# Projecting k and v by pairs of batches in the attention loops of a two-layer gated cross-attention kernel

## The reference, cut to what matters

```
x = x + tanh(g)*attention0(layernorm(x), ctx)      # 16 heads of 16 columns
x = x + tanh(g)*moe8(layernorm(x))                 # 8 experts with a capacity, top 1
x = x + tanh(g)*attention1(layernorm(x), ctx, ctx)
x = x + tanh(g)*moe4(layernorm(x))                 # 4 experts, top 2

# attention, for each batch:
q = layernorm(x) @ Wq ; k = ctx @ Wk ; v = ctx @ Wv
out = softmax(q k^T / 4) v @ Wo
```

## Time and profile before

| | value |
|---|---|
| time of the profiled execution | 2127.31 us |
| its span | 2125.5 us |
| TensorE busy | 2039.2 us (96%) |
| VectorE busy | 1756.2 us (83%) |
| ScalarE busy | 1496.7 us (70%) |
| GpSimd busy | 1217.2 us (57%) |
| 300 to 400 us (layer-0 attention): TensorE, VectorE, ScalarE, GpSimd | 97.91, 86.69, 63.84, 80.52 of 100 us |
| 1400 to 1500 us (layer-1 attention): the same | 100.00, 71.53, 67.27, 75.23 of 100 us |
| granted TensorE clock in both | 1.00 |
| DMA share in both | 0.22, 0.23 |

### The profile page before, as it was taken

The page is one execution under the profiler, slowest core; times in us unless marked ns, Lnnn a source line. Parts: engine busy times, 40 slices in busy tenths (PEclk is TensorE's granted clock), DMA queues, the critical chain, the costliest instruction groups (busy, mean ns, idle before and its releaser), DMA issues.

```text
span 2125.5 us, 57822 instructions
## 1 busy us (share of the span) xinstructions
PE 2039.2 (96%) x19788; PEld 1794.9 (84%) x19788; DVE 1756.2 (83%) x4916; ACT 1496.7 (70%) x3234; POOL 1217.2 (57%) x1800
## 2 busy tenths in 40 slices
PE   6999999999699999999799999999999999999997
PEld 5888888888599999999678888888788888888885
DVE  5889888898588888888677777777589999999996
ACT  4666666666478787878466666666668888888885
POOL 5788888878300000000277878877457777777776
PEclk9999999999799999999799999999999999999998
DMA  7555122221366666666422222222101100001000
GB/s 233 189 180 170 62 71 62 64 68 54 147 223 240 229 238 231 237 232 235 158 66 71 71 74 71 71 71 76 47 24 31 31 31 30 30 30 31 31 28 18
DMA packets 151665, 226.12 MB, mean 106 GB/s; under 512 B 20454, under 2 KB 135786, under 8 KB 141036
## 3 DMA queue, kind: packets, MB, share of 16 engines
q1 hardware_dynamic: 145260, 205.99, 28.8%
q0 software_dynamic: 6144, 16.79, 2.6%
HBM read 153.77 MB, written 68.94 MB: 105 GB/s over the span
## 4 chain that ended last, share of the span: by engine, by line
PE 87%; DVE 4%; issue 3%; DMA 2%; POOL 2%; ACT 1%; SPq 0%; POOLq 0%; ACTq 0%; DVEq 0%
PE ps L1254 11%; PE ps L1270 10%; PE ps L1126 10%; PE ps L1025 10%; PE ps L984 8%; PE ps L1111 6%; PE ps L1065 4%; PE ps L1202 3%; PE ps L1214 3%; PE ps L1158 3%; PE ps L1044 3%; PE ps L1059 2%; PE ps L1082 2%; PE ps L1095 2%; DMA slots_d<-rows,slot_s 2%
## 5 line engine op out<-in xcount | busy, mean ns | idle before, releaser
L1406 DVE TENSOR_REDUCE nmax<-ps 128x16 f32<-128x2048 f32 x128 | 292.4, 2284 | 29.7 <-PE ps L1082 29.3
L873 ACT ACTIVATE prob_t<-ps 128x2048 f32<-128x2048 f32 x128 | 240.9, 1882 | 77.5 <-PE ps L1065 77.5
L688 POOL COPY slot_in<-slot_all 128x1 int32<-128x1 int32 x64 | 11.4, 178 | 473.3 <-DMA eo_d<-eo 473.3
L1025 PE MATMUL ps<-w2f,a_t 128*128 128x256 f32 x1024 | 231.7, 379 | 0.3 <-ACT a_t L805 0.3
L1254 PE MATMUL ps<-xgt_hi,w_hl 128*128 128x256 f32 x1248 | 230.4, 283 | 1.0 <-DVE xgt_lo L1671 1.0
L1270 PE MATMUL ps<-w_hl,hid_hi 128*128 128x256 f32 x1248 | 226.9, 284 | 0.0
L1025 PEld LDWEIGHTS ps<-w2f,a_t 128*128 128x128 f32 x1024 | 189.6, 190 | 23.8 <-ACT a_t L805 0.6
L662 POOL TENSOR_TENSOR km_r<-qk,cst 128x512 fp32r<-128x512 f32 x128 | 133.5, 1043 | 126.1 <-ACT qk L863 126.1
L945 ACT ACTIVATE hid<-ps,b_in 128x256 f32<-128x256 f32 x312 | 146.1, 469 | 82.8 <-PE ps L1254 67.5
L1254 PEld LDWEIGHTS ps<-xgt_hi,w_hl 128*128 128x128 f32 x1248 | 195.7, 190 | 1.4 <-issue 1.4
L805 ACT ACTIVATE a_t<-ps,be_in,g_in 128x128 f32<-128x128 f32 x512 | 186.0, 470 | 12.2 <-PE ps L1044 11.3
(11 more groups left out here) (230 smaller groups left out, 6273.8 us busy)
## 6 DMA issues: line engine op xcount, KB each, us to landing
w_raw<-in_w_dram SPq DMA_DIRECT2D x78, 1024.0 KB, 6.8
c_t<-in_ctx_in_dram SPq DMA_DIRECT2D x128, 128.0 KB
x_d<-x SPq DMA_DIRECT2D x128, 128.0 KB, 2.4
slots_d<-zeros SPq DMA_DIRECT2D x12, 1024.0 KB, 6.1
eo_d<-zeros SPq DMA_DIRECT2D x12, 1024.0 KB, 5.6
xg<-slots_d SPq DMA_DIRECT2D x39, 256.0 KB, 2.8
eo_d<-eo SPq DMA_DIRECT2D x39, 256.0 KB, 2.2
x_in<-in_x_dram SPq DMA_DIRECT2D x64, 128.0 KB, 2.2
```

Source lines behind the costliest of these rows:

```text
L873: nc.scalar.activation(prob_t[:].rearrange("p a k -> p (a k)"), scores.rearrange("p a k -> p (a k)"), ACT.Exp, scale=SOFT).then_inc(y["exp ...
L1025: mm = pe.matmul(dst, a_t[:, b.parity, e, c, :], w2f[:, e, c, :], start=False, stop=True, skip_group_check=True)
L1406: nc.vector.tensor_reduce(nmax[:, b.parity, :, 0:4], scores.rearrange("p a (r k) -> p a r k", k=P), AX_X, ALU.max, negate=True).then_inc(y ...
```

## The change

- k is projected for two batches at once, with fp32r products of high and low parts: the weights `wk_hi` and `wk_lo` stand still and 256 columns (two batches) of `c_hi` or `c_lo` move. That is one group of twelve matmuls, at the end of the odd steps, for the batches s+1 and s+2.
- v is projected for two batches in one group of twelve matmuls, at the end of the even steps, for the batches s-2 and s-1. q stays as it was.
- `c_t`, `c_hi` and `c_lo` hold pairs. `c_hi` and `c_lo` are made every second step, 512 columns wide, two steps ahead.
- On ScalarE the turned rows `x_t` are copied first, then (even steps) the k pair or (odd steps) the v pair. q is copied by itself.
- On GpSimd `km_r` waits for the k copy only, `qm` for the q copy.
- `wk_hi` and `wk_lo` are made by ScalarE and VectorE at the start of each loop; TensorE waits for them.

```diff
...
@@ -222,9 +224,9 @@
-c_t = psb("c_t", [P, 4, C, P])
-c_hi = psb("c_hi", [P, 2, C, P], F32R)
-c_lo = psb("c_lo", [P, 2, C, P], F32R)
+c_t = psb("c_t", [P, 2, C, 2, P])
+c_lo = psb("c_lo", [P, 3, C, 2, P], F32R)
+c_hi = psb("c_hi", [P, 3, C, 2, P], F32R)
@@ -235,7 +237,8 @@
-qk = psb("qk", [P, 4, 4, P])
+q_in = psb("q_in", [P, 4, 2, P])
+k_in = psb("k_in", [P, 2, 2, 2, P])
...
@@ -524,11 +527,14 @@
-    b = s + 1
-    if b.within(B):
-        if (b - 4).begun:
-            sp.wait_ge(y["v_done"].of(b - 4), y["v_done"].at(b - 4))
-        sp.dma_start(c_t[:, b.off % 4].rearrange("p c k -> p (c k)"), row(ctx_in, b)).then_inc(y["c_came"].of(b), 16)
+    e = s + 3
+    if e.off % 2 == 0 and e.within(B):
+        if (e - 3).begun:
+            sp.wait_ge(y["c_lo_done"].of(e - 3), y["c_lo_done"].at(e - 3))
+        for t in range(2):
+            b = e + t
+            sp.dma_start(c_t[:, e.off // 2 % 2, :, t, :], row(ctx_in, b).rearrange("p (c k) -> p c k", c=C))\
+                .then_inc(y["c_came"].of(b), 16)
@@ -545,7 +551,7 @@
-        sp.wait_ge(s_wv[n], 2)
+        sp.wait_ge(s_wv[n], 4)
@@ -711,18 +717,18 @@
-        pool.wait_ge(y["qk_out"].of(b), y["qk_out"].at(b, 1))
-        masked(km_r[:, b.parity], qk[:, b.off % 4, 2:4, :]).then_inc(y["km_done"].sem, 1)
+        pool.wait_ge(y["k_out"].of(b), y["k_out"].at(b))
+        masked(km_r[:, b.parity], k_in[:, b.off // 2 % 2, :, b.off % 2, :]).then_inc(y["km_done"].sem, 1)
         if (b - 2).begun:
             pool.wait_ge(y["s2_done"].of(b - 2), y["s2_done"].at(b - 2))
-        masked(qm[:, b.parity], qk[:, b.off % 4, 0:2, :]).then_inc(y["qm_done"].sem, 1)
-    b = s - 1
-    if b.within(B):
-        pool.wait_ge(y["c_hi_done"].of(b), y["c_hi_done"].at(b))
-        if (b - 2).begun:
-            pool.wait_ge(y["v_done"].of(b - 2), y["v_done"].at(b - 2))
-        nc.gpsimd.tensor_tensor(c_lo[:, b.parity], c_t[:, b.off % 4], c_hi[:, b.parity], ALU.subtract)\
-            .then_inc(y["c_lo_done"].sem, 1)
+        pool.wait_ge(y["q_out"].of(b), y["q_out"].at(b, 1))
+        masked(qm[:, b.parity], q_in[:, b.off % 4]).then_inc(y["qm_done"].sem, 1)
+    e = s + 2
+    if e.off % 2 == 0 and e.within(B):
+        r = e.off // 2 % 3
+        pool.wait_ge(y["c_hi_done"].of(e + 1), y["c_hi_done"].at(e + 1))
+        nc.gpsimd.tensor_tensor(c_lo[:, r], c_t[:, e.off // 2 % 2], c_hi[:, r], ALU.subtract)\
+            .then_inc(y["c_lo_done"].sem, 2)
@@ -809,23 +815,31 @@
+nc.scalar.activation(wk_hi[:], w_k[:], ACT.Copy).then_inc(s_wv[n], 1)
 nc.scalar.activation(wv_hi[:], w_vp[:], ACT.Copy).then_inc(s_wv[n], 1)
 def step(s):
-    b = s - 3
-    if b.within(B):
-        act.wait_ge(y["v_done"].of(b), y["v_done"].at(b))
-        if (b - 2).begun:
-            act.wait_ge(y["av_done"].of(b - 2), y["av_done"].at(b - 2))
-        nc.scalar.activation(v_aug[:, b.parity, :, 0:DH], b5[:, 0:D].rearrange("p (h d) -> p h d", h=H),
-                             ACT.Copy).then_inc(y["v_out"].sem, 1)
     b = s
     if b.within(B):
         act.wait_ge(y["x_turned"].of(b), y["x_turned"].at(b))
         if (b - 1).begun:
-            act.wait_ge(y["qk_done"].of(b - 1), y["qk_done"].at(b - 1))
+            act.wait_ge(y["q_done"].of(b - 1), y["q_done"].at(b - 1))
         nc.scalar.activation(x_t[:].rearrange("p a k -> p (a k)"), b7[:, P:P + D], ACT.Copy)\
             .then_inc(y["x_t_done"].sem, 1)
+    e = s
+    if e.off % 2 == 0 and e.within(B):
+        act.wait_ge(y["k_done"].of(e + 1), y["k_done"].at(e + 1))
+        if (e - 3).begun:
+            act.wait_ge(y["s2_done"].of(e - 3), y["s2_done"].at(e - 3))
+            act.wait_ge(y["km_done"].of(e - 3), y["km_done"].at(e - 3))
+        nc.scalar.activation(k_in[:, e.off // 2 % 2].rearrange("p m t k -> p (m t k)"), b5, ACT.Copy).then_inc(y["k_out"].sem, 2)
+    e = s - 3
+    if e.off % 2 == 0 and e.within(B):
+        act.wait_ge(y["v_done"].of(e + 1), y["v_done"].at(e + 1))
+        if (e - 1).begun:
+            act.wait_ge(y["av_done"].of(e - 1), y["av_done"].at(e - 1))
+        nc.scalar.activation(v_aug[:, :, :, 0:DH], b5.rearrange("p (t h d) -> p t h d", t=2, h=H),
+                             ACT.Copy).then_inc(y["v_out"].sem, 2)
@@ -841,13 +855,15 @@
-    b = s - 1
-    if b.within(B):
-        act.wait_ge(y["c_came"].of(b), y["c_came"].at(b))
-        if (b - 2).begun:
-            act.wait_ge(y["v_done"].of(b - 2), y["v_done"].at(b - 2))
-        nc.scalar.activation(c_hi[:, b.parity].rearrange("p c k -> p (c k)"),
-                             c_t[:, b.off % 4].rearrange("p c k -> p (c k)"), ACT.Copy).then_inc(y["c_hi_done"].sem, 1)
+    e = s + 2
+    if e.off % 2 == 0 and e.within(B):
+        r = e.off // 2 % 3
+        act.wait_ge(y["c_came"].of(e), y["c_came"].at(e))
+        act.wait_ge(y["c_came"].of(e + 1), y["c_came"].at(e + 1))
+        if (e - 5).begun:
+            act.wait_ge(y["v_done"].of(e - 5), y["v_done"].at(e - 5))
+        nc.scalar.activation(c_hi[:, r].rearrange("p c t k -> p (c t k)"),
+                             c_t[:, e.off // 2 % 2].rearrange("p c t k -> p (c t k)"), ACT.Copy).then_inc(y["c_hi_done"].sem, 2)
@@ -856,15 +872,14 @@
-        act.wait_ge(y["qk_done"].of(b), y["qk_done"].at(b))
+        act.wait_ge(y["q_done"].of(b), y["q_done"].at(b))
         if (b - 4).begun:
-            act.wait_ge(y["s2_done"].of(b - 4), y["s2_done"].at(b - 4))
             act.wait_ge(y["qm_done"].of(b - 4), y["qm_done"].at(b - 4))
-        nc.scalar.activation(qk[:, b.off % 4].rearrange("p a k -> p (a k)"), b5, ACT.Copy).then_inc(y["qk_out"].sem, 1)
+        nc.scalar.activation(q_in[:, b.off % 4].rearrange("p a k -> p (a k)"), b5[:, 0:2 * P], ACT.Copy).then_inc(y["q_out"].sem, 1)
         if (b - 2).begun:
             act.wait_ge(y["s1_done"].of(b - 2), y["s1_done"].at(b - 2))
         nc.scalar.activation(q_r[:, b.parity].rearrange("p a k -> p (a k)"), b5[:, 0:2 * P], ACT.Copy)\
-            .then_inc(y["qk_out"].sem, 1)
+            .then_inc(y["q_out"].sem, 1)
...
@@ -1120,23 +1135,20 @@
-    def projections(w, part, src):
+    b = s
+    if b.within(B):
+        pe.wait_ge(y["x_t_done"].of(b), y["x_t_done"].at(b))
+        if b.off % 2 == 0:
+            pe.wait_ge(y["k_out"].of(b + 1), y["k_out"].at(b + 1))
+        elif (b - 2).begun:
+            pe.wait_ge(y["v_out"].of(b - 2), y["v_out"].at(b - 2))
+        else:
+            pe.wait_ge(y["q_out"].of(b - 1), y["q_out"].at(b - 1))
         for m in range(C):
             for c in range(C):
-                mm = pe.matmul(b5[:, (part + m) * P:(part + m + 1) * P], w[:, c, m * P:(m + 1) * P],
-                               src[:, c, :], start=(c == 0), stop=(c == C - 1))
-        return mm
-
-    b = s
-    if b.within(B):
-        pe.wait_ge(y["x_t_done"].of(b), y["x_t_done"].at(b))
-        if (b - 3).begun:
-            pe.wait_ge(y["v_out"].of(b - 3), y["v_out"].at(b - 3))
-        elif (b - 1).begun:
-            pe.wait_ge(y["qk_out"].of(b - 1), y["qk_out"].at(b - 1))
-        projections(w_q, 0, x_t)
-        pe.wait_ge(y["c_came"].of(b), y["c_came"].at(b))
-        projections(w_k, 2, c_t[:, b.off % 4]).then_inc(y["qk_done"].sem, 1)
+                mm = pe.matmul(b5[:, m * P:(m + 1) * P], w_q[:, c, m * P:(m + 1) * P], x_t[:, c, :],
+                               start=(c == 0), stop=(c == C - 1))
+        mm.then_inc(y["q_done"].sem, 1)
@@ -1202,18 +1214,29 @@
-    b = s - 2
-    if b.within(B):
-        if (b + 2).within(B):
-            pe.wait_ge(y["qk_out"].of(b + 2), y["qk_out"].at(b + 2))
-        else:
-            pe.wait_ge(y["v_out"].of(b - 1), y["v_out"].at(b - 1))
-        pe.wait_ge(y["c_lo_done"].of(b), y["c_lo_done"].at(b))
-        for c in range(C):
-            for ct, w in ((c_hi, wv_hi), (c_hi, wv_lo), (c_lo, wv_hi)):
-                mm = pe.matmul(b5[:, 0:D], ct[:, b.parity, c, :], w[:, c, :],
-                               start=(c == 0 and ct is c_hi and w is wv_hi), stop=(c == C - 1 and ct is c_lo))
-        mm.then_inc(y["v_done"].sem, 1)
+    if s.off >= 0 and (s.off % 2 == 0 or (s + 1).within(B)):
+        last = s if s.within(B) else At(0, B - 1)
+        pe.wait_ge(y["q_out"].of(last), y["q_out"].at(last))
+    e = s + 1
+    if e.off % 2 == 0 and e.within(B):
+        r = e.off // 2 % 3
+        pe.wait_ge(y["c_lo_done"].of(e + 1), y["c_lo_done"].at(e + 1))
+        for m in range(C):
+            for c in range(C):
+                for w, ct in ((wk_hi, c_hi), (wk_hi, c_lo), (wk_lo, c_hi)):
+                    mm = pe.matmul(b5[:, m * 2 * P:(m + 1) * 2 * P], w[:, c, m * P:(m + 1) * P],
+                                   ct[:, r, c].rearrange("p t k -> p (t k)"),
+                                   start=(c == 0 and w is wk_hi and ct is c_hi), stop=(c == C - 1 and w is wk_lo))
+            mm.then_inc(y["k_done"].sem, 1)
+    e = s - 2
+    if e.off % 2 == 0 and e.within(B):
+        r = e.off // 2 % 3
+        for t in range(2):
+            for c in range(C):
```

(25 more changed lines are left out.)

2 lines of the change are left out of this document (1 added, 1 removed).

## The result

The changed kernel takes 2143.91 us (median of 4 runs, 2141.45 to 2145.79) against 2127.14 (4 runs, 2124.65 to 2129.44): ratio 1.0078, 95% interval 1.0061 to 1.0096. Forecast were 2122 and a range of 2109 to 2134. The profiled execution has a span of 2139.5 us, 14.0 more than before.

A forecast was written before the change was run, and what follows sets the result against it. TensorE, near 98 to 100% busy, was taken as the bound, with VectorE's reduction as floor. Slot cycles -7.4, early steps -1.2, layer 1 +2.4, scatter -0.5, start +1.3 gave -5.4 us: 2122, range 2109 to 2134.

The forecast's parts named there:

- The floor of T: Both loops: T, the maxima transpose's weight load, waits for VectorE's reduction, so not before S (maximum scores' start) + 2.98 us.
- Layer 0's plain step: Layer 0, steps without slot calculation: 7.87 us each, 0.13 less than before.
- The term for the nine early steps: Layer 0, nine steps before the slot work starts: -0.13 us each, -1.2 us in all.
- Layer 1's step: Layer 1, each step: 7.47 us, 0.04 longer than before; +2.4 us over some 60 steps.
- from T to L1158 is 1.55 us ... so 4.49: Layer 1: stretch from the maxima transpose to the next step's start, 4.49 us instead of 4.55 when the transpose is waited for.
- The slot step: Layer 0, step with VectorE's slot calculation: bn_stats at S + 6.75 instead of 7.74; 0.57 us less a cycle, -7.4 us.
- qm from when ScalarE has copied q (about 3.9 ...) to 5.0: Layer 0's slot step, GpSimd layout: qm starts after ScalarE's q copy, about S + 3.9, and ends at 5.0.
- the lower bound of this term: Layer 0's slot cycle if GpSimd is never in VectorE's way: 3 x 7.87 + 8.03 = 31.64 us, -1.34 a cycle.
- The start: Start of layer 0: one more ScalarE copy and VectorE subtraction ahead of the first bn_stats, +1.3 us; layer 1, 0.
- The scatter's wait: Layer 0: scatter issued 1 to 2 us earlier, ending VectorE's wait for its landing; -0.5 us over the loop.
- ScalarE's copies: Both loops: the rearranged, wider copies cost nothing; if 0.2 us later, 0.1 a second step, 6 us in all.
- The rival that came true: VectorE's chain is the loop: reduction floor binds each step, slot chain hardly shortens; 2136 us, chance 0.25.

The follow-up runs named there:

- e1: Changed kernel, with GpSimd's km_r also waiting for VectorE's xh of the same step; 2129.62 us, ratio 1.0013.
- e2: Changed kernel with three buffers for qm instead of two; 2123.50 us, ratio 0.9984.
- b2: Kernel before the change with only ScalarE's order changed, x_t copied in front of v_aug; 2129.33 us, ratio 1.0003.
- e7: Changed kernel with three qm buffers, layer 1's o_pad turn ahead of the maxima's, and ScalarE's wide copy back in front of x_t; 2114.60 us, ratio 0.9937.
- b1: Kernel before the change with three buffers for qm instead of two and nothing else; 2127.79 us, ratio 0.9996.
- e4: Changed kernel; in layer 1 alone TensorE's turn of o_pad stands ahead of the turn of the row maxima; 2148.03 us, ratio 1.0097.
- e6: Changed kernel with three qm buffers, layer 1's early o_pad turn, and layer 0's context pairs split one step earlier; 2123.07 us, ratio 0.9974.

## Why the prediction was wrong, by its steps

- **The floor of T** was right: S + 2.97 or 2.98 in the plain steps of layer 0 and in 52 of 63 steps of layer 1. In layer 1 it has the reduction as releaser, with 0.19 us of wait where I had said some 0.28. In the other eleven T is S + 3.20 to 3.47. Two of these are the first of the loop, and nine lie behind VectorE's one-off weight work, which I had called covered and which is not.
- **Layer 0's plain step**, 7.87: right to the hundredth. The term for the nine early steps was not: -1.2 forecast, -0.1 measured from 56.78 to 113.58, since one of them (from 104.91) took 8.66 in place of 8.00. No run tells why.
- **Layer 1's step**, 7.47: right in even steps (7.42), wrong in odd ones (7.78). The step that failed is "from T to L1158 is 1.55 us ... so 4.49": I took the stretch behind T as TensorE's work alone. It holds a wait for VectorE in each odd step. Term: +2.4 forecast, +9 measured. e1 and e2 each bring the odd step back to 7.46.
- **The slot step.** It is the sentence "qm from when ScalarE has copied q (about 3.9 ...) to 5.0". The copy was there at S + 3.6, but the buffer was free only at S + 4.72. Term: -7.4 forecast, 0 measured. With the wait removed (e2) bn_stats is at S + 6.47, earlier than the forecast 6.75, and the cycle is shorter by 1.0, more than the forecast 0.57. c_lo cost 1.30, not 1.04. The 8.03 in the lower bound of this term has no working: by the prediction's own 5.09 from T to S, the third step was to be about 8.23, as it is in every trace, and the bound 31.84, not 31.64.
- **The start**: +1.3 forecast, +5.1 measured. The first S is 1.3 later (19.95 against 18.68), as forecast, though not by the forecast work alone: the first bn_stats is 2.0 later (11.81 us against 9.81), because wk_lo took 1.75 us beside GpSimd's c_lo, where it took 0.68 in e2. There bn_stats is at 9.85 and the first S at 18.46, no later than before, and the sixth S is still at 55.35. So the other 3.9 lie in the first steps: 7.38, 7.80 and 6.76 us, where they were 4.45, 6.63 and 7.01. I priced the preparation and left out these steps: the first now holds a k pair of 2.5 us behind the turn of xh, and stretches of low clock lie in both. How much each costs is not shown.
- **The scatter's wait**, -0.5: about right. VectorE waited for the scatter seven times before (4.5 us between 56 and 540 us) and twice after (1.7 us); the ten cycles behind the S of step 21 took 330.4 us before and 329.8 after.
- **ScalarE's copies**: nothing, and nothing was found (b2, e7). TensorE shows 0.17 us for v_aug at L1126, but the same 0.17 stands there without v.
- **The rival that came true** is the slower one: it put its decision at bn_stats later than S + 7.3, and it came at 7.42. Its layer-1 term (+0.10 a step) had the wrong mechanism, and its 2136 is 8 us under the measured time too.

The rule of the Trainium skill that I weighed (SBUF — State Buffer, section "Who interferes with whom") was the right place to look, and I applied it to the slot calculation only, not to xh, which had been 0.43 us and which km_r would now meet. The traces agree that xh is blocked: 1.74, 1.24 and 2.13 us where GpSimd was busy, 0.40 where it was idle. They show more than one blocking instruction can explain: the 1.74, 2.13 and 3.01 each ran across two or more GpSimd instructions that followed one another.

That one wait caused both steady losses is shown by e2, and that the change made it by b1. That xh is held by GpSimd's instructions is read from their times and from e1, e4 and e6. That nmax_x and the turn behind it pass xh's delay on to TensorE is shown by the chain of waits (1.13 us against 0.81) and by e1, where a short xh and a short odd step come together while the pairs and qm's two buffers stay. What the start costs in parts stays open.

## What to carry to other kernels

When an edit lets an operation go earlier, list every wait of the operations behind it in its queue, the waits for a free buffer too: one that never ended last before can end last now, and it delays all that follows on that engine into the next step. In this kernel what counted was less how much GpSimd did than where its gaps lay: two GpSimd operations without a gap held a VectorE instruction for both, four of them for 3.01 us. And an edit that loses alone (the early turn, +4 us) may be the one that pays once another cause is gone.
